# Between two scans of a gated delta-rule layer: the forget gate's four products moved in between the output projection's tiles, and one key projection moved ahead of the routing's gates

## The reference

```
x = x + 0.5 * ffn(layernorm(x))
x = x + attn(layernorm(x))
x = x + 0.5 * ffn(layernorm(x))

attn:  q, k, v = silu(x @ Wq), silu(x @ Wk), silu(x @ Wv)      # 8 heads of 32
       log_f   = log_sigmoid(x @ Wf1 @ Wf2)                     # the forget gate, rank 32
       beta    = sigmoid(x @ Wbeta) * 2
       k       = k / sqrt(sum(k*k) + eps)                       # per head
       per token: S = exp(log_f) * S, then the delta-rule update with k, beta, v;  o = q @ S
       y = o * sigmoid(x @ Wog1 @ Wog2);  y = y / rms(y) * norm_w;  out = y @ Wo
ffn:   p = softmax(x @ router_w.T); the two best of 8 experts; each gated, weighted and added
```

## Time and profile before

| | |
|---|---|
| median of 3 runs | 1869.19 us |
| time of the profiled execution | 1866.42 us |
| its span in the profile | 1864.6 us |
| PE busy | 1593.2 us (85%) |
| DVE busy | 1126.5 us (60%) |
| ACT busy | 774.5 us (42%) |
| POOL busy | 760.1 us (41%) |
| mean granted clock of PE | 0.932 of full |
| start and length of stretch 1, 2, 3 up to the end of job 7 | 711 to 763, 942 to 994, 1176 to 1229 us |

### The profile page before, as it was taken

One profiled execution on the slowest core, in us unless ns is written; L12 is line 12 of the kernel. 1 busy time (PEld: TensorE's weight loads), 2 busy tenths in 40 slices (PEclk: granted clock), 3 DMA queues, 4 the chain that ended last, 5 costly groups with the idle time before them and its releaser, 6 DMA issues. The chain is left out here.

```text
span 1864.6 us, 69187 instructions
## 1 busy us (share of the span) xinstructions
PE 1593.2 (85%) x26524; PEld 1302.6 (70%) x26525; DVE 1126.5 (60%) x3424; ACT 774.5 (42%) x1805; POOL 760.1 (41%) x944
## 2 busy tenths in 40 slices
PE   5499999999577988788888788887885999999994
PEld 5499999999435565355654556545564999999994
DVE  7646434444357786877868778688774546444341
ACT  2143333333267334673346733467332443333331
POOL 2554422222154651646516465164651234422221
PEclk9999999999779898798987999889897999999997
DMA  9563433232300200002000020000102833332334
GB/s 300 184 187 76 88 48 48 45 51 45 74 4 7 70 22 24 4 7 70 22 23 4 7 70 23 23 4 7 47 23 83 255 78 76 75 64 47 49 48 113
DMA packets 84233, 116.23 MB, mean 62 GB/s; under 512 B 12952, under 2 KB 74464, under 8 KB 82016
## 3 DMA queue, kind: packets, MB, share of 16 engines
q1 hardware_dynamic: 56160, 74.17, 13.1%
q0 software_dynamic: 27360, 37.80, 11.5%
q10 hardware_dynamic: 608, 2.96, 0.5%
HBM read 64.87 MB, written 54.21 MB: 64 GB/s over the span
## 5 line engine op out<-in xcount | busy, mean ns | idle before, releaser
L1065 POOL DMA_INDIRECT x<-ffn_yout,ffn_place x142 | 222.6, 1568 | 531.6 <-DVE ffn_yout L997 454.6
L1003 DVE TENSOR_TENSOR ffn_inner<-ffn_inner,ffn_bank 128x512 f32<-128x512 f32 x142 | 97.6, 687 | 349.2 <-PE ffn_bank L873 346.8
L873 PE MATMUL ffn_bank<-ffn_tileT,ffn_gate_now 128*128 128x128 f32 x2272 | 280.2, 277 | 0.0
L873 PE MATMUL ffn_bank<-ffn_tileT,ffn_up_now 128*128 128x128 f32 x2272 | 277.6, 275 | 0.0
L954 ACT ACTIVATE ffn_inner<-ffn_bank 128x512 f32<-128x512 f32 x142 | 84.8, 597 | 459.0 <-PE ffn_bank L873 459.0
L883 PE MATMUL ffn_bank<-ffn_w,ffn_inner 128*128 x1136 | 268.9, 380 | 1.7 <-DVE ffn_yout L997 1.7
L873 PEld LDWEIGHTS ffn_bank<-ffn_tileT,ffn_gate_now 128*128 128x128 f32 x2272 | 268.4, 194 | 0.1
L873 PEld LDWEIGHTS ffn_bank<-ffn_tileT,ffn_up_now 128*128 128x128 f32 x2272 | 266.1, 193 | 0.0
L883 PEld LDWEIGHTS ffn_bank<-ffn_w,ffn_inner 128*128 128x128 f32 x1136 | 205.0, 190 | 24.4 <-issue 2.5
L816 ACT COPY ffn_gate_now<-ffn_w 128x1024 f32 x142 | 148.4, 1045 | 29.9 <-issue 22.3
L816 DVE COPY ffn_up_now<-ffn_w 128x1024 f32 x142 | 99.6, 702 | 55.3 <-issue 43.9
(11 more groups left out here) (574 smaller groups left out, 3179.3 us busy)
## 6 DMA issues: line engine op xcount, KB each, us to landing
ffn_w<-in_w1t_dram SPq DMA_DIRECT2D x16, 1024.0 KB, 5.6
ffn_tile<-xs SPq DMA_DIRECT2D x122, 130.0 KB, 2.1
ffn_w<-in_w2t_dram SPq DMA_DIRECT2D x16, 512.0 KB, 6.9
at_a_sb<-x SPq DMA_DIRECT2D x32, 256.0 KB, 2.8
ffn_x<-in_x_dram SPq DMA_DIRECT2D x16, 256.0 KB, 5.5
x<-ffn_x SPq DMA_DIRECT2D x16, 256.0 KB, 6.1
x<-at_a_sb SPq DMA_DIRECT2D x16, 256.0 KB, 2.1
xs<-ffn_empty SPq DMA_DIRECT2D x23, 130.0 KB, 2.9
```

Source lines behind the costliest of these rows:

```text
L873: t = pe.matmul(bank[:, i * P:(i + 1) * P], half_now[half][b][:, k, i * P:(i + 1) * P], rowsT[b][:, k * P:(k + 1) * P], start=(k == 0), st ...
L1003: dve.tensor_tensor(inner[b][:, :], inner[b][:, :], p_u[b][:, :], ALU.mult).then_inc(s_act, 1)
L1065: pool.indirect_dma_start(total, bass.IndirectOffsetOnAxis(ap=place[b][:, 0:1], axis=0), yout[b][:, :], None, compute_op=ALU.add).then_inc ...
```

## The change

All of it is in `between`. The four forget products no longer stand behind the eighth output tile: one stands behind each second tile, so that three of them are ahead of the last two tiles. Job 0, the first key projection, no longer stands behind the routing's rounds but ahead of them. So that job 0 does not write into bank 0 or 1, which the routing's transposes use, it goes to bank 2, jobs 1 and 2 to banks 0 and 1, job 4 to bank 0; job 5 in bank 2 then waits for four silus and not three. In the call for pass 0 nothing moves, only the banks differ. The last call is unchanged.

```
-    JOB_BANKS = (0, 1, 2, 0, 1, 2, 3, 2)
-    BANK_FREE = (0, 0, 0, 1, 2, 3, 0, 6)
+    JOB_BANKS = (2, 0, 1, 2, 0, 2, 3, 2)
+    BANK_FREE = (0, 0, 0, 1, 2, 4, 0, 6)
...
+                def forget(j):
+                    g, c = QUARTERS[j]
+                    pe.wait_ge(s_fgc, 2)
+                    if ends:
+                        pe.wait_ge(s_ly, j + 1)
+                    pe.matmul(psum[4 + j][:, :], wrank[0:RANK, g * P:(g + 1) * P], fg[0:RANK, c * 512:(c + 1) * 512],
+                              start=True, stop=True).then_inc(s_f, 1)
...
                         t.then_inc(s_wo, 1)
+                        if begins and i % 2 == 1:
+                            forget(i // 2)
+                if begins and not ends:
+                    for j in range(4):
+                        forget(j)
                 if begins:
-                    pe.wait_ge(s_fgc, 2)
-                    for j, (g, c) in enumerate(QUARTERS):
...
+                    job(0)
                 if routes:
                     r.gate_tensor(pe, 0)
                 if begins:
-                    for j in range(4):
-                        job(j)
+                    job(1)
+                    job(2)
+                    job(3)
                 if routes:
                     r.count_tensor(pe, 0)
```

More of the change, by code:

```diff
@@ L1379, in _ @@
                         t.then_inc(s_wo, 1)
-                if begins:
-                    pe.wait_ge(s_fgc, 2)
-                    for j, (g, c) in enumerate(QUARTERS):
[L1383 to L1386, removed]
+                        if begins and i % 2 == 1:
[3 more added lines that the diff above has]
+                        forget(j)
+                if begins:
+                    job(0)
                 if routes:
```

## The result

The changed kernel takes 1879.33 us (median of five runs, 1877.17 to 1886.85) against 1869.19 us for the kernel before on the same chip (1866.24 to 1870.12). The ratio is 1.0073, with a 95% interval from 1.0056 to 1.0090, so it is slower by 10.5 to 16.8 us. I had leaned to slower, but by 3.7 us, and my range ended at 1877.5.

The account below looks back on a forecast made before the run. It took each stretch as bounded by the routing's rounds' start, the rounds, and DVE's way to L335. 6.75 - 2.8 - 1.36 + 1.1 = +3.7 us on 1869.19 gave 1872.9 us, range 1867.5 to 1877.5.

Parts of the forecast that it names:

- Step 1: Output projection on PE: three forget products ahead of the last tiles start the routing's rounds 2.25 us later per stretch, +6.75 us.
- Step 2: Routing's rounds: job 0 ahead of them keeps PE's clock at the upper level for 4 rounds per stretch, -2.8 us.
- Step 3: Behind the rounds: one job less on PE brings DVE's awaited counts sooner, gaining only in stretch 1, -1.36 us.
- Step 4: DVE's way to L335: silus and POOL's squares come sooner and lengthen DVE's steps, 1.5 us per stretch, +1.1 us net.
- longer than 0.40: Sign on PE ahead of job 6: PE still waits for L335, for more than 0.40 us.
- that case: Rival on PE's clock: upper level holds through all eight rounds, 7.5 us gained in place of 2.8, 1868.2 us; chance 0.17.
- The change does what it says: Rival behind the rounds: PE ends last, so job 0's 1.72 us count in every stretch, sum -0.1, 1869.1 us; chance 0.07.
- The squares' full block: Rival on the SBUF port: POOL's squares block DVE's two-operand steps fully, sum +6.7, 1875.9 us; chance 0.15.
- The clock not held: Rival in the routing's rounds: job 0 does not keep PE's clock up at all, sum +9.2, 1878.4 us; chance 0.12.

Follow-up runs that it names:

- `pairs_only`: Kernel before, with two forget products behind every four output tiles, job 0 and banks as before: ratio 1.0038 to the kernel before, +7.1 us.
- `job0_between`: Job 0 between the fourth and fifth output tile, all forget products behind the tiles as in the kernel before: one run, +10.4 us against the kernel before.
- `after_again`: The changed kernel run once more, unaltered, for a second profile: ratio 1.0064 to the kernel before, +12.0 us.
- `forget_only`: Kernel before with only the forget products moved between the output tiles; job 0 left behind the rounds, banks as before: ratio 1.0039, +7.3 us.
- `before_hold`: Kernel before, with POOL's squares held back until the slots are made (L335): ratio 1.0001 to the kernel before, +0.2 us.
- `after_fill`: Changed kernel plus two extra 128-row products, read by nobody, ahead of PE's wait for L335: ratio 1.0047 to the kernel before, +8.8 us.
- `after`: The changed kernel itself, in its first profile: 1879.33 us median, ratio 1.0073 to the kernel before; the profiled execution took 1886.85 us.
- `job0_only`: Changed kernel's job 0 move and banks only; forget products behind the eighth output tile as in the kernel before: ratio 1.0026, +4.9 us.
- `job0_hold`: Job 0 ahead of the rounds, forget products behind the eighth tile, POOL's squares held until L335: ratio 0.9983 to the kernel before, -3.2 us.
- `split_hold`: Forget products behind the eighth tile, job 0 between the second and third, ahead of the rounds, squares held until L335: ratio 1.0008, +1.5 us.

## Why the prediction was wrong

| step of the prediction | forecast, us | in the first pair of profiles, us |
|---|---|---|
| 1: rounds start later | +6.75 | +10.19 |
| 2: clock in the rounds | -2.8 | -3.58 |
| 3: wait for the counts in stretch 1 | -1.36 | -1.36 |
| 4: squares against DVE | +1.1 | +4.69 |
| no step: clock in the wait for L335 | 0 | +3.00 |
| sum | +3.7 | +12.94 |

**Step 1 failed in its size, by 3.4 us.** "Three forget products ahead of the last tiles" at 0.86 us each took the price from four that stand in a row. In a row the height changes once at either end; spread out, each product brings two changes of 0.19 us. `pairs_only` and `job0_between` show this. The Trainium skill (TensorEngine Tiling (Array Packing), Key Properties) says that a change of tiling mode "drains the TensorE", and gives no price. The products over 32 rows among those over 128 behave like such a change, which I had not weighed. I had also written "no bound below it", but gave no bound above it either; that was the mistake in kind.

**Step 2 was right.** Job 0 held the clock into the rounds, for 2.4, 4.1 and 4.5 us of them, and the gain was 3.58 for 2.8 (4.47 in `after_again`). PE idled 0.67 us behind job 0, where I had 0.9. `forget_only` shows the same rounds without it (30.0 us against 25.4).

**Step 3 was right for the counts, by a reading that was wrong in part.** In no stretch after does DVE wait for the counts. The table's -1.36 is that wait, and the rest of the way is step 4's. But I had written that PE sat idle for L335 "in every stretch". In stretch 1 of before it did not: jobs 5, 6 and 7 follow one another without a gap, and job 6 starts at 759.34, 0.36 us behind the end of L335. Three of the five records of the earlier trace rows are weight loads.

```profile
757.62 5.31 PE L1344 MATMUL at_wide<-at_gt,at_wq 128*128 128x512 f32 x12
```

So in that stretch PE was last, and `before_hold` agrees: without the squares the way stays 13.14 us. How the shorter and the longer part of that stretch's way are divided between steps 3 and 4 is bookkeeping.

**Step 4 failed in its size, by 3.6 us.** The way less 11.03 us was 0.74 (without the 1.36), 1.36 and 1.46 in before, 3.6 in all, near the 3.4 I read. After, it was 2.67, 3.00 and 2.58, 8.25 in all, where I took 1.5 each and had 2.5 as the upper end. I saw that the first square would meet L269, but counted "the nearest rows" of before, where squares fell beside short steps of DVE and met one or two of them. Now the squares of both jobs 0 and 1 start a moment ahead of L269 and L270, 0.77 and 0.80 us, and the other two still meet something. In `after_again` the ways less 11.03 us are 7.26 in all, so the step was +3.7 there: a miss of 2.6 to 3.6. My value of 1.5 went by how many squares there are. What counted was which of the two starts first. The rival drawn from the Trainium skill (SBUF — State Buffer, SBUF: two separate sides), that the later one fully blocks, was nearer than my value: with squares of 1.04 us that started 0.12 and 0.09 us earlier, a full block is 0.92 and 0.95 us, the trace shows 0.77 and 0.80. So the trace agrees with it but for 0.15 us.

**The step I did not have: +3.0 us.** I wrote that PE would wait for L335 "longer than 0.40", and it did, up to 2.6 us, as two right steps meet: one job less behind the rounds, and a longer way on DVE. I charged nothing for it since PE was not what ended last. But its clock is: a wait makes no one late by itself, and the jobs behind it were on the path. `after_fill` removes it with work that nobody needs. In the four profiles with an early job 0 and neither hold nor fill (`after`, `after_again`, `job0_only`, `job0_between`), waits of 2.5 to 2.6 us had this effect in eight of nine cases, those of 2.1 us in none of three.

**The rivals.** The clock did hold better than forecast, but not by the 4.7 us that case needed. "The change does what it says" is out: after the change PE waited for L335 in every stretch. The squares' full block was right in its place and at +4.69 even beyond its price; the time that went with it, 1875.9 us, lies 3.4 below the median, as much as step 1 lacked. The clock not held is out. That its 1878.4 us came nearest to the 1879.33 is luck: what it priced did not happen.

## What to carry to other kernels

Price a product that is moved between others of a different height with the change on either side of it, and read that price from a place where they alternate. Work that is moved ahead to fill an idle engine also moves what it sets off: here a silu and a square that met DVE's longest steps; one wait on the engine that does them gave back 10 to 12 us of the stretches. Where an engine with a clock gate is left waiting longer, charge the work behind the wait at the lower level, even if the wait itself costs nothing.

## What the runs showed of the hardware that I had not expected

- A change between products over 32 rows and products over 128 rows costs some 0.19 us of PE, though its timeline shows no idle time (1.05 us for 0.86, 1.93 for 1.75).
- PE's granted clock can fall while PE is busy without a gap, inside the four 32-row products: in all three stretches of `job0_hold`, in one of the kernel before, in none of `job0_only`. It did not where job 0 parted them into two times 1.9 us (`split_hold`).
- It fell at the end of PE waits of 2.57 to 2.58 us and, 1.4 us later, behind one of 2.47 us (`job0_only`, stretch 1); it stayed up behind one of 2.52 us (`after_again`, stretch 2) and those of 2.11 to 2.13 us.
- A step of DVE over 128x512 with two operands in SBUF that starts some 0.1 us behind a 1.04 us square on POOL takes 0.77 to 0.81 us longer. Steps with one operand are lengthened too, L272 from 0.19 to 0.52 us (`after`, stretch 1) and L301, a copy of 128x8, from 0.17 to 1.02. Where the square started 0.30 us behind L270 (before, stretch 2), the square took 1.29 us and L270 its 0.69.
